# Two quarters earlier on VectorE, the block product at a round's end on TensorE, with six transposes of the identity ahead of it

## What is computed

```
def gat_conv(x, src, dst, W, att_src, att_dst, bias, n_nodes):
    h = (x @ W).reshape(n_nodes, Hh, Cc)
    a_src = (h * att_src).sum(-1)
    a_dst = (h * att_dst).sum(-1)
    alpha = leaky_relu(a_src[src] + a_dst[dst])
    m = jax.ops.segment_max(alpha, dst, num_segments=n_nodes)
    e = jnp.exp(alpha - m[dst])
    denom = jax.ops.segment_sum(e, dst, num_segments=n_nodes)
    w = e / jnp.clip(denom, 1e-16)[dst]
    out = jax.ops.segment_sum(w[:, :, None] * h[src], dst, num_segments=n_nodes)
    return out.reshape(n_nodes, Hh * Cc) + bias
...
x = _layernorm(x + L0(x))   # two gat_conv of 4 heads, relu between, each node also its own neighbour
x = _layernorm(x + L1(x))   # a linear layer, then one such layer of 8 heads without own edges
```

## Time and profile before

| | us |
|---|---|
| median of 3 runs | 6530.64 (6526.72 to 6537.1) |
| the profiled execution's own time | 6552.36 |
| its span, first to last instruction | 6550.3 |
| rounds 12 to 95 (the loop), layer 0, 1, 2 | 1777.9, 1795.6, 1768.7 |
| TensorE array busy | 4781.3 (73%) |
| VectorE busy | 4564.3 (70%) |
| GpSimd busy | 4532.0 (69%) |
| ScalarE busy | 2734.9 (42%) |

### The profile page before, as it was taken

How to read it: one execution, slowest core, us unless ns; L and a number is a source line. 1 busy time by engine, 2 the same in 40 slices (tenths; PEclk the granted TensorE clock), 3 DMA queues, 4 the chain that set the end, 5 groups by cost and what they waited for, 6 DMA issues and landing times. The chain is left out here.

```text
span 6550.3 us, 105533 instructions
## 1 busy us (share of the span) xinstructions
PE 4781.3 (73%) x21848; PEld 3433.9 (52%) x21849; DVE 4564.3 (70%) x13234; ACT 2734.9 (42%) x4932; POOL 4532.0 (69%) x4736
## 2 busy tenths in 40 slices
PE   6777777777777577777777777765776777677776
PEld 5555555555555455555555555544555555555555
DVE  6666666666666667777777777766766776677676
ACT  3343444344344334444444444433444444444443
POOL 2777777777777477767777777737777777777774
PEclk8788888888878778878887888877998999989898
DMA  8555555555555355555555555535555555555553
GB/s 271 146 149 150 148 152 147 149 149 149 148 148 150 99 150 163 162 155 159 160 159 158 162 159 159 162 105 150 158 156 152 153 156 156 149 156 154 153 154 97
DMA packets 477595, 1000.76 MB, mean 153 GB/s; under 512 B 143755, under 2 KB 284975, under 8 KB 476654
## 3 DMA queue, kind: packets, MB, share of 16 engines
q0 software_dynamic: 226208, 633.50, 36.6%
q1 hardware_dynamic: 250574, 356.73, 17.1%
HBM read 918.52 MB, written 71.30 MB: 151 GB/s over the span
## 5 line engine op out<-in xcount | busy, mean ns | idle before, releaser
L867 POOL DMA_INDIRECT e_rows<-table,loaded x4689 | 4513.6, 963 | 1883.7 <-issue 1670.9
L1160 PE MATMUL e_p_mm<-e_rows,e_onehot 128*128 128x264 f32 x9378 | 2762.9, 445 | 139.3 <-DVE e_rows L1354 109.2
L1160 PEld LDWEIGHTS e_p_mm<-e_rows,e_onehot 128*128 128x128 f32 x9378 | 1973.5, 219 | 555.4 <-issue 203.7
L1354 DVE TENSOR_TENSOR e_rows<-e_rows,e_p_pair 128x1024 f32<-128x1024 f32 x1173 | 1413.6, 1205 | 0.0
L1622 DVE TENSOR_TENSOR_SCAN e_fwd<-e_mask,e_p_one 64x128 f32<-64x128 bf16 (+1 forms) x294 | 121.9, 415 | 1294.4 <-PE e_p_one L1250 1294.4
L1346 DVE TENSOR_TENSOR e_onehot<-e_col,e_p_pair 128x512 f32<-128x512 f32 (+1 forms) x1176 | 903.1, 768 | 79.3 <-issue 76.1
L1250 PE MATMUL e_p_one<-ident,e_srcc 128*64 128x128 f32 (+1 forms) x294 | 91.2, 310 | 1006.9 <-issue 644.4
L997 ACT ACTIVATE e_onehotT<-e_onehotT,minus_pidx 128x2432 bf16<-128x2432 bf16 x294 | 680.8, 2316 | 21.2 <-DMA e_pass<-pass_rows 21.2
L1000 ACT ACTIVATE e_onehotT<-e_onehotT,one_col 128x2432 bf16<-128x2432 bf16 x294 | 682.6, 2322 | 9.6
L1250 PEld LDWEIGHTS e_p_one<-ident,e_srcc 128*64 128x64 f32 (+1 forms) x294 | 36.8, 125 | 1120.1 <-issue 1120.1
L1152 PE MATMUL e_p_mm<-e_rows,e_onehot 128*128 x1764 | 469.5, 402 | 208.9 <-DVE e_rows L1354 207.7
(11 more groups left out here) (323 smaller groups left out, 5384.7 us busy)
## 6 DMA issues: line engine op xcount, KB each, us to landing
e_onehotT<-rel_rows SPq DMA_DIRECT2D x294, 608.0 KB
e_rows<-table,loaded POOLq DMA_INDIRECT x4689
e_own_row<-table SPq DMA_DIRECT2D x196, 128.0 KB, 3.2
table<-e_rows_out SPq DMA_DIRECT2D x98, 132.0 KB, 2.7
table<-n_rows_out SPq DMA_DIRECT2D x14, 910.0 KB, 13.8
table<-e_rows_out SPq DMA_DIRECT2D x98, 130.0 KB, 3.0
n_inputs<-in_x_turned SPq DMA_DIRECT2D x14, 896.0 KB, 10.7
e_mask<-mask_rows SPq DMA_DIRECT2D x196, 64.0 KB
```

The source lines that it names most:

```text
L867: pool.indirect_dma_start(rows[k][:, g, 0:TW], None, table[L], bass.IndirectOffsetOnAxis(ap=idx[k][:, g:g + 1], axis=0)).then_inc(s_gat[k] ...
L1160: ins = nc.tensor.matmul(p_mm[:, bass.ds(region, MW)], onehot[:, g, :], rows[k][:, g, :], start=False, stop=True, skip_group_check=True)
L1354: return nc.vector.tensor_tensor(feats, feats, p_e[:, gs, :].unsqueeze(3).to_broadcast([P, n, H, C]), ALU.mult)
```

## The change

On VectorE the third quarter is worked on behind the second, before the carried maxima are read, and the fourth before the logits instead of behind `fdist`. On TensorE, extras and products(3) follow products(2) directly, then come fmat, `turn` and `multiply`. `multiply` now takes the block that was turned in the same round (w - 6, not w - 7), so its wait for `xT` is for the copy of the turn just before, and ahead of the product it transposes the identity six times into the product's own space, which the product then overwrites. It is gone from behind srcT. ScalarE copies the turned block behind `factor` instead of ahead of it. In the first round of each pass of the loop (u = 0, behind the jump) the four loads of words stand behind srcT (and behind `last_sums` in layer 2). The order of TensorE's queue is then: words, srcT, rowsum, lookups, products(0), colsum, products(1), topT, products(2), words, extras, products(3), fmat, turn, six turns of the identity, the product. The layer's end has one step of its loop less.

```
--- before.py
+++ after.py
@@ -1111,11 +1111,11 @@
                     nc.scalar.activation(rows[k][:, :, D:D + H], gap[:], ACT.Exp).then_inc(st["erow"], 1)
                     wait(act, st["msg3"], past)
                     nc.scalar.activation(p_e, gap[:], ACT.Exp).then_inc(st["expo"], 1)
-                    if CARRY and finished(w, 6):
-                        take_turned(w, u)
                     act.wait_ge(st["fmat"], now)
                     wait(act, st["rescaled"], past)
                     nc.scalar.activation(factor[:], p_small[:, MAT_AT:MAT_AT + H], ACT.Exp).then_inc(st["factor"], 1)
+                    if CARRY and finished(w, 6):
+                        take_turned(w, u)
                 if CARRY:
                     act.wait_ge(s["w"], 16 * (2 if NORMED else 3))
                 walk(act, body)
@@ -1212,12 +1212,16 @@
                         nc.tensor.matmul(p_node[:, D:2 * D], turned[:, c, :], lin[:, c, :], start=False, stop=False)
                     nc.tensor.matmul(p_node[:, D:2 * D], slope_ident, vin[:], start=False, stop=True).then_inc(s["mm"], 1)
 
+                IDLE_TURNS = 6
+
                 def multiply(w, u):
 
-                    r = (u - 7) % TURNS
-                    wait_apart(pe, s["xT"], place_of(pe, w, 7))
-                    if finished(w, 8):
-                        wait_apart(pe, s["row"], place_of(pe, w, 8))
+                    r = (u - 6) % TURNS
+                    wait_apart(pe, s["xT"], place_of(pe, w, 6))
+                    if finished(w, 7):
+                        wait_apart(pe, s["row"], place_of(pe, w, 7))
+                    for _ in range(IDLE_TURNS):
+                        nc.tensor.transpose(p_node[:, 0:P], ident[:], ident[:])
                     for c in range(2):
                         nc.tensor.matmul(p_node[:, 0:WA], turned_x[r][:, c * P:(c + 1) * P], wmat[:, c, :], start=c == 0, stop=False)
                     nc.tensor.matmul(p_node[:, 0:WA], sum_parts[:], bias_parts[:], start=False, stop=True).then_inc(s["mm"], 1)
@@ -1236,11 +1240,18 @@
                 def body(w, u, i, ago, first):
                     k, two = u % BUFS, u % TURNS
                     now, past = ago(0), ago(1)
-                    if not first:
-                        regions = words(pe, REGION_ROW, (w - 1) * G, G, (REGIONS - 1) * BANK)
-                    offs = words(pe, AD_ROW, w * G, G, (PLACES - 1) * ADS_W)
-                    flag, *extra_ad = words(pe, WINDOW_ROW, w * WIN + W_FLAG, 1 + EXTRAS, (PLACES - 1) * ADS_W)
-                    slots = words(pe, WINDOW_ROW, w * WIN + W_TILE, EXTRAS, G - 1)
+
+                    def round_words():
+
+                        regions = None if first else words(pe, REGION_ROW, (w - 1) * G, G, (REGIONS - 1) * BANK)
+                        offs = words(pe, AD_ROW, w * G, G, (PLACES - 1) * ADS_W)
+                        flag, *extra_ad = words(pe, WINDOW_ROW, w * WIN + W_FLAG, 1 + EXTRAS, (PLACES - 1) * ADS_W)
+                        slots = words(pe, WINDOW_ROW, w * WIN + W_TILE, EXTRAS, G - 1)
+                        return regions, offs, flag, extra_ad, slots
+
+                    behind_jump = u == 0 and not isinstance(w, int)
+                    if not behind_jump:
+                        regions, offs, flag, extra_ad, slots = round_words()
                     def products(q):
                         if not first:
                             for g in range(4 * q, 4 * q + 4):
@@ -1251,8 +1262,8 @@
                                         ).then_inc(st["srcT"], 1)
                     if LINEAR and finished(w, 5):
                         last_sums(w, u, i)
-                    if CARRY and finished(w, 7):
-                        multiply(w, u)
+                    if behind_jump:
+                        regions, offs, flag, extra_ad, slots = round_words()
                     wait_apart(pe, st["scan"], now)
                     wait_apart(pe, st["factor"], past)
                     for dst, col, o in ((0, fwd[:, P - 1:P], 0), (1, bwd[:, 0:1], P)):
@@ -1275,18 +1286,17 @@
                     products(1)
                     wait_apart(pe, st["top"], now)
                     nc.tensor.transpose(p_top[:, 0:HG], seg[:], ident[0:HG, 0:HG]).then_inc(st["topT"], 1)
+                    products(2)
+                    if not first:
+                        extras((k - 1) % BUFS, words(pe, WINDOW_ROW, (w - 1) * WIN + W_TILE, EXTRAS, G - 1), past)
+                    products(3)
+                    wait_apart(pe, st["fdist"], now)
+                    nc.tensor.matmul(p_small[:, MAT_AT:MAT_AT + H], first_row[:], fdiff[:], start=True, stop=True
+                                     ).then_inc(st["fmat"], 1)
                     if CARRY and finished(w, 6):
                         wait_apart(pe, st["topread"], now)
                         turn(w, u)
-                    products(2)
-                    if not first:
-                        old_slots = words(pe, WINDOW_ROW, (w - 1) * WIN + W_TILE, EXTRAS, G - 1)
-                    wait_apart(pe, st["fdist"], now)
-                    nc.tensor.matmul(p_small[:, MAT_AT:MAT_AT + H], first_row[:], fdiff[:], start=True, stop=True
-                                     ).then_inc(st["fmat"], 1)
-                    if not first:
-                        extras((k - 1) % BUFS, old_slots, past)
-                    products(3)
+                        multiply(w, u)
                 if CARRY:
                     pe.wait_ge(s["w"], 16 * (2 if NORMED else 3))
                     pe.wait_ge(s["prep_pe"], 1)
@@ -1295,7 +1305,6 @@
                     last_sums(WINDOWS, WINDOWS % UNROLL, WINDOWS // UNROLL)
                 if CARRY:
                     pe.wait_ge(st["topread"], W0 + WINDOWS)
-                    multiply(WINDOWS, WINDOWS % UNROLL)
                     turn(WINDOWS, WINDOWS % UNROLL)
                 regions = words(pe, REGION_ROW, (WINDOWS - 1) * G, G, (REGIONS - 1) * BANK)
                 old_slots = words(pe, WINDOW_ROW, (WINDOWS - 1) * WIN + W_TILE, EXTRAS, G - 1)
@@ -1309,10 +1318,11 @@
                 pe.sem_inc(s_mm[3], 1)
                 for q in range(LAST_TILES // 4, 3):
                     pe.sem_inc(s_mm[q], 1)
-                for w in range(WINDOWS + 1, BLOCKS + 8) if CARRY else ():
+                if CARRY:
+                    multiply(WINDOWS, WINDOWS % UNROLL)
+                for w in range(WINDOWS + 1, BLOCKS + 7) if CARRY else ():
+                    turn(w, w % UNROLL)
                     multiply(w, w % UNROLL)
-                    if finished(w, 6):
-                        turn(w, w % UNROLL)
                 if LINEAR:
                     pe.wait_ge(s["chain"], 2)
                     for half in range(2):
@@ -1656,6 +1666,7 @@
                     nc.vector.tensor_tensor_scan(flat(outb)[:, ::-1], pass_b[:, ::-1], flat(inb)[:, ::-1], -BIG,
                                                  ALU.add, ALU.max).then_inc(st["carry"], 1)
                     quarters(1)
+                    quarters(2)
                     dve.wait_ge(st["carry"], now)
                     nc.vector.tensor_tensor(nxt[:], outf[:, :, G - 1:G], passes[two][:, 1, :, 0:1], ALU.add).then_inc(st["tail_sum"], 1)
                     dve.wait_ge(st["lookup"], now)
@@ -1670,7 +1681,7 @@
                     dve.wait_ge(st["top1"], now)
                     nc.vector.scalar_tensor_tensor(seg[:], m[0:HG, 3, :], p_small[0:HG, COLS_AT + 1:COLS_AT + 2], seg[:], ALU.add, ALU.max
                                                    ).then_inc(st["top"], 1)
-                    quarters(2)
+                    quarters(3)
                     dve.wait_ge(st["adst"], now)
                     nc.vector.tensor_tensor(l1, rows[k][:, :, D:D + H], adst[:], ALU.add)
 
@@ -1697,7 +1708,6 @@
                     dve.wait_ge(st["first_d"], now)
                     nc.vector.scalar_tensor_tensor(fdiff[:], m[0:1, 0, 0:1].to_broadcast([1, H]), -1.0, fd[:], ALU.is_ge, ALU.mult
                                                    ).then_inc(st["fdist"], 1)
-                    quarters(3)
                     if CARRY:
                         carried(w, u, i)
                     else:
```

54 lines of the change are left out of this document (26 added, 28 removed).

## The result

The changed kernel takes 6875.7 us (median of 4 runs, 6874.6 to 6881.2) beside 6528.9 us of the kernel before on the same chip (4 runs): a ratio of 1.053, 95% interval 1.0515 to 1.0549. It is slower, by 347 us; 6860 was predicted, within 6690 to 7000. The profiled execution took 6875.0 us, its span is 6873.0. That of the kernel before took 6552.4 us, 22 us above its own median and above all the runs of that kernel beside it, so the two spans differ by 323 us only.

What follows compares the result with a forecast made beforehand. The prediction took a chain from VectorE's last quarter through TensorE's sequencer and its register loads as the bound. Terms 190 + 179 + 17 + 6 - 42 = +350 gave about 6880, taken as 6860 us, range 6690 to 7000.

Steps and rivals of the forecast that it cites:

- The bound: All layers: the chain from VectorE's last quarter through TensorE's sequencer, 4.9 us of register loads, sets the 20.6 us round.
- The ordinary round: Layers 0 and 1, timed from srcT's start (S): loads queue behind the product's wait, 23.0 us against 20.6, 2.4 longer.
- The jump: Loop's end, layers 0 and 1: jump round 22.4 and 22.9 us, next round 26.2 with 3.2 charged for moved loads.
- Rounds before the loop: Five rounds with the product ahead of the loop in layers 0 and 1: +1.7 us each, +17 for both.
- Layer ends: Seven blocks pass turn, copy, turns and product in sequence, less one loop step: +3 us each, +6.
- Layer 2: No block product there, so gathers set the pace at 123 us a pass: -42 us, with 0 and -88 as ends.
- a jump round without extra idle time: Sign expected in layer 2's changed profile, beside rounds of 20.4 us; the branch was to be covered.
- doubtful terms: Whole sum: each had more room below than above, so 6860 us was taken instead of about 6880.
- A: Faster rival: gathers set the pace in all layers and all jumps are hidden, 6355 us; chance 8%.
- B: Milder rival: short loads of 4.2 us and full array clock in layers 0 and 1, 6665 us; chance 13%.
- C: Heavier rival: half clock moves to the round's end, 7190 us for a third of rounds, 7025 for a sixth; chance 9%.
- D: Rival: moved loads don't help; layer 2 gains 20 to 40 us, +2 in 28 jumps, 6900 to 6940; chance 8%.

Runs made afterwards that it cites:

- e5: Kernel before with VectorE's quarters sooner, extras and fourth products ahead of fmat and turn; product still behind srcT, words at round's head, no turns: 6297.0 us, 0.964.
- e7: e5 with the words of each pass's first round loaded behind srcT and the product: 6372.5 us, 0.976.
- e6: The changed kernel without the six identity turns ahead of the block product: 6849.8 us, 1.049.
- e12: Kernel before with only the words of the round behind the loop's jump moved behind srcT and the product: 6562.9 us, 1.006.
- e8: Kernel before with an unused sixteen-word load that was dropped from the program, so a second trace of the kernel before: ratio 0.9994, span 6516.5 us.
- e3: Kernel before with an unused sixteen-word load that was dropped from the program, run on the chip that takes 10172 us: ratio 1.0003.

## Why the prediction was right

The medians of the runs take the change apart in four steps, each on top of the one before: order -232 (e5, 6297.0 less 6528.9), words behind the jump +75 (e7), product at the round's end +477 (e6), identity turns +26 (the changed kernel). They add up to the whole change by construction, which is no evidence for them. In another order of steps they can differ, as the words behind the jump do: +38 in the order of the kernel before, +75 in that of e5.

**The bound.** Right. One used load more costs 1.24 us in each round of the kernel before, with nothing else changed. In e5 it costs 0.45. Two figures were read or worked out a little off: the four loads of the round in the earlier trace rows take 4.76 us and not 4.9, and their mean in the loop of layer 0 is 4.4 us, 4.3 in the changed kernel, so they gain 0.1 us of the 0.4 that I let them gain; and 22 instructions of 0.035 us are 0.77 us, not 0.6 to 0.7.

**The ordinary round.** In the round shown, against the prediction: fourth quarter S + 11.7 (11.8), extras 13.0 (12.5), turn's end 17.0 (16.5), identity turns 17.95 (17.65), words 18.1 (18.3), srcT 22.8 (23.0). The array was half a microsecond later than I had it. The sequencer made up for it: it began the loads 0.1 to 0.2 us after the first identity turn, where I had counted 0.6 to 0.7 for turns and product. From the first load to srcT it is 4.7 us, 4.8 predicted. So the two errors cancel, and that the sum of this round came out so near is in part luck. The mean of the 56 ordinary rounds of layer 0 is 22.9 us, also in layer 1.

**The jump.** The round that ends in it takes 22.8 and 22.7 us in layers 0 and 1 (22.4 and 22.9 predicted), the round behind it 26.0 and 25.7 (26.2); first products at S + 8.0 (8.3). A pass of layer 0 is 140.4 (140.6), of layer 1 139.9 (141.1); the 0.5 us that I added to layer 1's jump were not there. I had charged 3.2 us for the moved loads against 4.3 saved, so a small gain; e7 and e12 show a loss, 75 and 38 us by the medians. In the order of the changed kernel itself the move was not tried alone.

**The small terms.** Three were mis-sized. Rounds before the loop: +17 predicted, +2.2 measured in both layers together. I counted the five rounds with a product and forgot the six without, which gain from the new order: in layer 0 rounds 1 to 6 take 3.6 us less. The five with a product, rounds 7 to 11, take 4.6 us more there, about half of the 8.5 that I had. Layer ends: +6 predicted, +2.2 measured. Layer 2: -42 predicted, -27.8 in the loop and -5.3 before it. e5 has -51.3 in that loop, with the words at their old place; there the mechanism gives more than I took. The sign "a jump round without extra idle time" failed in layer 2: the ordinary rounds take 20.1 us there, but the round behind the jump takes 23.7 in the changed kernel and 22.3 in e6. Why these 1.4 us a pass come and go between kernels with the same instructions in layer 2 stays open.

**The sum.** On the profiled executions +350 stands against +322.6: too high by 27: 3 and 16 in the loops of layers 0 and 1, 15 before them, 4 at the ends, less 8 in layer 2 with its first rounds and end, and 2 in the last rounds. On the medians the change is +347. So part of the agreement is luck: the base of the sum, the kernel before, was 22 us longer in its profiled execution than in the median. Measured against e8's trace instead, the loops are +200, +173 and -21 us against the +190, +179 and -42 predicted, and the spans differ by 356 us. The sum itself gave 6880, 4 us from the 6875.7 measured; the 20 us that I took off for doubtful terms were not there.

**The rivals.** A, gathers as the pace, did not happen in layers 0 and 1 of the changed kernel but does in e5, less clearly in its layer 2: 6297 us, under the 6355 that I worked out, because a pass can be 121.2 us. B had loads of 4.2 us, near the measured, but first products took 3.88 us as before. C: in the rounds shown the turn takes 0.44 us and the product 1.06 for its 2.10 in e5, so the half clock did not move to the end of the round; the granted clock fell from 0.82 to 0.79, and the 165 us or more of C did not appear. D: right that the moved loads don't help (why not, no run shows); in layer 2 some 8 us of the forecast gain are missing, far less than the 40 to 80 that D adds to the time.

**The Trainium skill.** The jump took 3.72 us here too. The Trainium skill, page "Advanced Engine Details and Errata", section "Control Flow Timing", gives about 108 ns for a compare-and-branch. TensorE's jump back is far from that, the other branches at this line are below it. In the changed kernel the 39 branches of TensorE that are taken last 3.5 to 5.8 us; the last one of each layer, behind which there is no jump, lasts 0.08 us, and the branches of the other four queues at L824 0.04 to 0.06 us. Why TensorE's jump takes so much longer, no run here shows.

## What to carry to other kernels

A wait in an engine's queue delays everything behind it, also what needs nothing from the engine itself. Here four register loads, 4.3 us together, had been free to run under the array's work; a product whose operand comes from a transpose of the same round was put ahead of them, and they start at S + 18.1 instead of the S + 13.8 that the rest of the change allows: an ordinary round that takes 20.0 us in e5 takes 22.9. Put what depends on nothing ahead of a wait and what depends on the newest result a round later, and test the pace with one more used instruction on the suspected queue.

Of the changed kernel, take the quarters and the order and leave the product behind srcT of the next round: 6297 us.

## What the hardware showed beside that

A register load of TensorE's sequencer from an SBUF tile takes 0.5 to 1.6 us in the rounds shown, and one of sixteen words cost 1.24 us where it lay on the path. The Trainium skill gives about 1.3 us for such loads from HBM at a launch (page "Runtime: NRT & Kernel Launch", section "The ~15µs preamble/postamble breakdown"), which the sixteen-word load is near.

One chip took 10172 us for the kernel that takes 6529 elsewhere, in 19 runs. VectorE and GpSimd are busy about as long there (4561 and 4475 us in e3), TensorE longer (5820 us); VectorE waits 3700 us for the lookups, ended by a semaphore that the view calls remote (waits of the whole span of e3):

```profile
DVE e_adst L1663 <- remote: 3704.8, 285, 31.4
```

In the trace of the kernel before, from another chip, VectorE's waits for the lookups are 4.4 us in all. The kernel without turns had a ratio of 0.926 on the first chip and of 1.049 on the other: the verdict on a change can differ in sign by the chip. Why was not found.
